# Local-attention layers: the feed-forward one pair of blocks later, its input matmuls behind the value matmuls, gelu behind the copies of the output

## The reference, cut to what matters

```
for i in range(DEPTH):                                     # DEPTH = 6
    x = attn_layer(shift_tokens(x), Wqkv[i], ...) + x
    x = ffn_layer(shift_tokens(x), ln_g[i], ln_b[i], W1[i], b1[i], W2[i], b2[i]) + x

def ffn_layer(x, g, bln, W1, b1, W2, b2):
    mu = x.mean(-1, keepdims=True)
    var = ((x - mu) ** 2).mean(-1, keepdims=True)
    xn = (x - mu) / jnp.sqrt(var + 1e-05) * g + bln
    a, gate = jnp.split(xn @ W1 + b1, 2, -1)               # 341 columns each
    return a * jax.nn.gelu(gate, approximate=False) @ W2 + b2
```

## Time and profile before

| | |
|---|---|
| median of 3 runs | 7343.36 us (7342.56 to 7348.19) |
| profiled execution, own time | 7338.15 us |
| its span, first to last instruction | 7336.3 us |
| stretch of the six layers | about 2741 to 7222 us |
| busy share of the span | PE 75%, DVE 63%, ACT 45%, POOL 36% |
| mean granted TensorE clock | 0.858 |

### The profile page before, as it was taken

One profiled execution on the slowest core, in us unless ns is written; L12 is line 12 of the kernel. 1 busy time (PEld: TensorE's weight loads), 2 busy tenths in 40 slices (PEclk: granted clock), 3 DMA queues, 4 the chain that ended last, 5 costly groups with the idle time before them and its releaser, 6 DMA issues. The chain is left out here.

```text
span 7336.3 us, 228324 instructions
## 1 busy us (share of the span) xinstructions
PE 5478.9 (75%) x94991; PEld 3176.4 (43%) x95226; DVE 4621.9 (63%) x9757; ACT 3311.9 (45%) x6753; POOL 2637.1 (36%) x2351
## 2 busy tenths in 40 slices
PE   5777877454777746888888888888888888888874
PEld 1222222112232214555555555555555555555552
DVE  5666666345555545676676666666666766666764
ACT  1444444121333313555555555555555555555542
POOL 0000000000000005555555555555555555655550
PEclk9999999576898967888888888888888888888885
DMA  3011010002111101001100110011001100110000
GB/s 95 14 20 20 13 20 14 26 0 84 27 20 26 20 8 52 23 23 29 32 23 23 29 32 23 23 29 32 23 23 31 34 23 23 31 29 23 23 19 18
DMA packets 99949, 197.56 MB, mean 27 GB/s; under 512 B 23616, under 2 KB 50048, under 8 KB 99328
## 3 DMA queue, kind: packets, MB, share of 16 engines
q1 hardware_dynamic: 94944, 195.44, 10.3%
q10 hardware_dynamic: 4896, 0.84, 0.1%
HBM read 67.45 MB, written 27.26 MB: 13 GB/s over the span
## 5 line engine op out<-in xcount | busy, mean ns | idle before, releaser
L340 DVE TENSOR_REDUCE a_mpart<-a_pm 128x1 f32<-128x512 f32 (+2 forms) x1904 | 1087.4, 628 | 511.9 <-PE a_pm L412 316.7
L517 ACT ACTIVATE a_probs<-a_ps 128x1024 f32<-128x1024 f32 (+3 forms) x896 | 796.0, 930 | 1123.5 <-PE a_ps L433 856.2
L1219 ACT ACTIVATE w_probs<-w_pa,w_nm,w_rqs 128x64 f32<-128x64 f32 x3072 | 971.2, 415 | 126.3 <-DVE w_nm L1367 124.4
L412 PE MATMUL a_pm<-a_KZ,a_QS 128*128 128x512 bf16 (+3 forms) x1869 | 665.1, 390 | 301.9 <-DVE a_mpart L340 187.7
L1212 ACT ACTIVATE w_sq<-w_pr 128x512 f32<-128x512 f32 x768 | 466.2, 607 | 898.4 <-DVE w_sinb L1355 898.4
L324 POOL COPY a_V<-a_vals 128x288 f32 x32 | 14.5, 452 | 1913.0 <-PE a_po L449 1911.7
L1141 PE MATMUL w_pr<-w_xc,w_w 128*128 128x256 f32 (+1 forms) x1152 | 455.6, 576 | 293.9 <-issue 293.9
L433 PE MATMUL a_ps<-a_QS,a_KS 128*128 128x512 bf16 (+3 forms) x1688 | 514.9, 379 | 140.9 <-DMA a_KS<-k_parts 118.1
L929 POOL TENSOR_TENSOR w_sinb<-w_sinb,w_tabk 128x512 f32<-128x512 f32 x384 | 488.4, 1272 | 283.8 <-DVE w_sinb L1355 283.8
L955 POOL TENSOR_TENSOR w_probs<-w_probs,w_rden 128x512 f32<-128x512 f32 x384 | 392.9, 1044 | 539.0 <-DVE w_rden L1377 539.0
L1355 DVE STREAM_SHUFFLE w_sinb<-w_pr 128x512 f32<-128x512 f32 x768 | 562.6, 733 | 0.0
(11 more groups left out here) (218 smaller groups left out, 10160.9 us busy)
## 6 DMA issues: line engine op xcount, KB each, us to landing
w_Vp<-w_V SPq DMA_DIRECT2D x192, 384.0 KB, 3.7
w_Vp<-w_V SPq DMA_DIRECT2D x192, 128.0 KB, 3.4
a_QS<-q_parts SPq DMA_DIRECT2D x136, 96.0 KB, 3.4
a_KZ<-k_parts SPq DMA_DIRECT2D x136, 96.0 KB, 3.6
a_KS<-k_parts SPq DMA_DIRECT2D x136, 96.0 KB, 3.7
q_parts<-a1p_part SPq DMA_DIRECT2D x48, 128.0 KB, 1.8
k_parts<-a1p_part SPq DMA_DIRECT2D x48, 128.0 KB, 1.8
q_parts<-a2p_part SPq DMA_DIRECT2D x48, 128.0 KB, 1.8
```

The lines of the kernel that those rows point to most:

```text
L340: nc.vector.reduce_max(mpart[:, h, qt, kc:kc + 1], p_m[:, k % 2, 0:width], AX_X).then_inc(max_read, 1)
L412: mm = nc.tensor.matmul(out, QS[:, par, h, qt * P:(qt + 1) * P], KZ[:, par, h, kc * CH:kc * CH + width], start=True, stop=True)
L517: nc.scalar.activation(probs[:, s % 2, 2 * pair:2 * pair + 2, c0:CH], p_s[:, pair, :, c0:CH], ACT.Exp, scale=SM_SCALE).then_inc(exped, 1)
L1219: op = nc.scalar.activation(probs[:, g, t, c, :], s_of(g)[:, t, c, :], ACT.Exp, bias=nm[:, g, t, c:c + 1], scale=scale_of(g)[:, t, c:c + 1])
```

## The change

The feed-forward (`ffn_in`, `gelu`, `gate`, `ffn_out`, `second_residual`) is done for pair n-3 instead of n-2 in turn n; output projection and layer norm stay at n-2. The flag `finish` is split into `mixing` and `feed`. TensorE does `ffn_in` behind `values`, ScalarE does `gelu` behind `keep_out`, and centre, variance, squares and layer norm stand a little later in their orders. A new tile xo keeps the normalized input between the turns; the first residual is written into XS in place of the tile x1, which drops one small instruction and its wait (L1387). vecn holds the two layer-norm vectors apart, with a load of its own. Turn 2 is now written out ahead of the loop, which repeats turns 3 to 93, and a turn 98 is added at the end.

```diff
 def turn(n, attend, mixing, feed, late, early):      # TensorE
     if mixing:
         mix(n - 2, attend)
     if late:
         unit(7, n)
-    if finish:
-        centre(n - 2)
-    if late:
-        norms(n)
-    if finish:
-        variance(n - 2)
-    if late:
-        turn_norms(n)
-    if finish:
-        ffn_in(n - 2, late, attend)
-    if late:
-        turn_back(n, finish)
+        norms(n)
+    if mixing:
+        centre(n - 2)
+    if late:
+        turn_norms(n)
+    if mixing:
+        variance(n - 2)
+    if late:
+        turn_back(n, mixing)
     if attend:
         values(n - 1)
+    if feed:
+        ffn_in(n - 3, 0, late, attend)
+        ffn_in(n - 3, 1, late, attend)
     if late:
-        spread_norms(n, finish)
+        spread_norms(n, feed)
         project_v(n)
-    if finish:
-        ffn_out(n - 2, late)
+    if feed:
+        ffn_out(n - 3, late, mixing)
...
 def spread_norms(m, after_ffn):
-            pe.wait_ge(S[("gl01", "hid2", "hid")[k]], m - 1 + FIRST)
+            pe.wait_ge(S[("gl01", "hid2", "hid")[k]], m - 2 + FIRST)
...
 def turn(n, attend, mixing, feed, late, early):      # ScalarE
     if attend:
         exps(3, 0, n - 1)
         exps(3, 1, n - 1)
-    if finish:
-        gelu(n - 2)
     if attend:
         keep_out(n - 1)
+    if feed:
+        gelu(n - 3)
     if late:
         keep_v(n)
...
 def residual(m):                                     # VectorE
-    dve.wait_ge(S["x2"], m + PPL + FIRST)
-    nc.vector.tensor_tensor(x1[64:128, 0:1], x1[64:128, PAIR:PAIR + 1],
-                            notfirst[64:128, ds(m % PPB, 1)], ALU.mult).then_inc(S["x1p"], 1)
-    dve.wait_ge(S["x1p"], m + 1 + FIRST)
     dve.wait_ge(S["y"], m + 1 + FIRST)
...
+def scale_norm(m):
     dve.wait_ge(S["xn1"], m + 1 + FIRST)
+    dve.wait_ge(S["f2"], m + FIRST)
+    dve.wait_ge(S["vecn"], m // PPL * 16 + 16)
-    nc.vector.tensor_scalar(xc[:, :], xc[:, :], vecs[:, 0:1], vecs[:, 1:2], ALU.mult,
+    nc.vector.tensor_scalar(xo[:, :], xc[:, :], vecn[:, 0:1], vecn[:, 1:2], ALU.mult,
                             ALU.add).then_inc(S["xn"], 1)
...
+    if mixing:
+        var_term(n - 2)
+        layer_norm(n - 2)
     if attend:
         denominator(1, n - 1)
...
-    if finish:
-        gate(n - 2)
+    if feed:
+        gate(n - 3)
+    if mixing:
+        scale_norm(n - 2)
     if late:
         scale_k(n)
```

More of the change, by code:

```diff
@@ L883, in _ @@
                     if l:
+                        sp.wait_ge(S["xn"], m0 + FIRST)
+                        load_n(l)
+                        sp.wait_ge(S["f2"], m0 + FIRST)
+                        load_1(l)
+                    carry_v(m0 + 2)
+                    shift_v(m0 + 2)
+                    if l:
                         sp.wait_ge(S["x2"], m0 + PPL + FIRST)
                         load_2(l)
-                    with sp.Fori(0, PPL - 3) as i:
-                        carry_v(i + (m0 + 2))
-                        shift_v(i + (m0 + 2))
+                    with sp.Fori(0, PPL - 4) as i:
+                        carry_v(i + (m0 + 3))
+                        shift_v(i + (m0 + 3))
                     if l + 1 < DEPTH:
@@ L956, in scale_probs, with turn @@
                                             ALU.mult).then_inc(S[f"pn{g}"], 1)
-                def turn(n, attend, finish, late, early, more=True):
+                def turn(n, attend, late, early, more=True):
                     if late:
@@ L980, in _ @@
                 table_k(1)
[L981 to L987, removed]
+                turn(0, False, True, True)
+                turn(1, True, True, True)
+                turn(2, True, True, True)
+                with nc.Fori(0, PAIRS - 5, engines=bass.OrderedEngineSet([pool.engine]), hint_back_edge=True) as i:
+                    turn(i + 3, True, True, True)
+                turn(PAIRS - 2, True, True, True, more=False)
+                turn(PAIRS - 1, True, True, False)
+                turn(PAIRS, True, False, False)
             @block.tensor
@@ L1125, in variance, with ffn_in @@
                     pe.wait_ge(S["xsq"], m + 1 + FIRST)
-                    nc.tensor.matmul(p_c[:, 0, :], ones[:, :], xsq[:, :], start=True, stop=True).then_inc(S["var"], 1)
-                def ffn_in(m, late, attend):
-                    pe.wait_ge(S["w1"], m // PPL * 16 + 16)
-                    pe.wait_ge(S["xn"], m + 1 + FIRST)
-                    for what, k, bank, at in FFN:
+                    nc.tensor.matmul(p_c[:, 1, :], ones[:, :], xsq[:, :], start=True, stop=True).then_inc(S["var"], 1)
+                def ffn_in(m, part, late, attend):
+                    if part == 0:
+                        pe.wait_ge(S["w1"], m // PPL * 16 + 16)
+                        pe.wait_ge(S["xn"], m + 1 + FIRST)
+                    for what, k, bank, at in FFN[3 * part:3 * part + 3]:
                         if at == 0:
                             if late:
-                                pe.wait_ge(S[("sq7", "n2c", "nrm")[bank]], m + 3 + FIRST)
+                                pe.wait_ge(S[("sq7", "n2c", "nrm")[bank]], m + 4 + FIRST)
                             elif attend:
@@ L1154, in ffn_out, with turn @@
                     mm.then_inc(S["out"], 1)
-                def turn(n, attend, finish, late, early):
+                def turn(n, attend, mixing, feed, late, early):
                     if attend:
```

139 lines of the change are left out of this document (74 added, 65 removed).

## The result

The changed kernel takes 7883.78 us (median of 4 runs, 7879.63 to 7887.56) against 7344.3 for the kernel before beside it: a ratio of 1.0734, 95% interval 1.0718 to 1.075. Slower by 540 us. The forecast was +616 for the profiled execution, which took 549 more: 7887.35, with a span of 7885.5, and the mean granted clock fell from 0.858 to 0.823.

The account below looks back on a forecast made before the run. No engine is full; engines wait for each other in a turn. 44.96 + 5.17 + 1.5 + 0.3 = 51.93, 596 us over 93 turns plus 20: +616, 7960 us; range 7780 to 8110, likeliest case 7870 to 8030.

Parts of the forecast that it names:

- The likeliest case: Whole loop: a turn between 51 and 53 us, forecast total 7960 us; chance 0.55.
- Front half: Ahead of the values: last transposition over at T+27.0, 3.5 of ffn_in's 4.22 us becoming a wait, values ending 0.7 earlier.
- The chain: Behind the values: copies 2.05, table load 1.28, gelu 1.20, gate 1.25, hand-overs 0.2; scale_k 5.17 us later, at T+35.9.
- rival (d): Table load right behind the copies: holds ScalarE longer, at most 1.28 us a turn, 119 more, 8079 us; chance 0.06.
- Ffn_in, 2.85 expected: TensorE behind the values: ffn_in takes 2.85 us, over at T+32.5, hidden behind the table load.
- The clock: TensorE's clock falling behind idle stretches: 1.5 us a turn on project_v, 0.3 on the values.
- what would show it: Signs in the new profile, among them keep_out about 0.7 us earlier, scale_k at T+35.9, a turn of 52 us.
- Rival (b): Between ffn_in and project_v: the clock holds through the thin stretch, turn 50.13 us, total 7792 us; chance 0.2.
- (c): Clock falls both ahead of the values' second half and of project_v: turn 54.03 us, total 8154 us; chance 0.14.
- Behind scale_k: From scale_k to the next turn: 14.23 us, taken as unchanged.
- the forecast's 6.41: Whole loop: new turn 51.93 against the mean 45.52, 6.41 us more a turn, 596 over 93 turns.
- The ends: First turns and last turns outside the steady loop: together 20 us more.

Follow-up runs that it names:

- e7: e5 with GpSimd scaling the first two groups of probabilities ahead of its last rotate: 7228.74 us, ratio 0.9856.
- e10: The changed kernel with only GpSimd's scaling of the first two groups of probabilities moved ahead of its last rotate: 7790.45 us, ratio 1.0617.
- e1: The kernel before with only gelu moved behind keep_out, ffn_in still ahead of the values: 8046.43 us, ratio 1.0958.
- e5: The changed kernel with ffn_in ahead of turn_back and gelu ahead of keep_out, delay by one pair kept: 7453.97 us, ratio 1.0159.
- e2: The changed kernel with the gelu table load ahead of keep_out, gelu itself still behind: 7861.6 us, ratio 1.0708.
- e3: The changed kernel with table load and gelu both ahead of keep_out, ffn_in still behind the values: 7862.9 us, ratio 1.0712.
- e4: The changed kernel with ffn_in back ahead of turn_back and the values, gelu still behind keep_out: 8077.61 us, ratio 1.1003.
- e12: e4 plus six extra matmuls a turn right behind the values, results never read: 7868.72 us, ratio 1.0718.
- e6: The changed kernel with three layer-norm operations moved behind keep_parts: 7854.82 us, ratio 1.0713.
- e11: e7 with e6's move of three layer-norm operations behind keep_parts: 7123.18 us, ratio 0.9712.
- e9: The changed kernel plus eight unread matmuls a turn, five ahead of turn_back, three between the halves of the values: 8171.89 us, ratio 1.1137.

## Why the prediction was right, and which step was off

The likeliest case came, and its main term for its reason: the chain copies, load, gelu, gate stands open behind the values. That the total came within 67 us is partly luck: scale_k stands 0.6 later than forecast, clock included, and what follows it is 1.3 shorter, because the price of the clock came in another place. Step by step:

- **Front half.** The floor was to come at T+17.0 and came at T+16.33; GpSimd was to hold the transpositions, and does: second one over at T+19.83 (forecast T+19.8), turn_back at T+21.92 (T+21.8), last one over at T+26.72 (T+27.0). e7 and e10 show that it is GpSimd's order. The forecast called 3.5 a wait in the middle of the values, though its own times give 2.1 there (T+24.9 to T+27.0); 0.59 came, and 4.70 of idle ahead of them.
- **The chain.** From the start of the copies to scale_k 6.17; the terms of the forecast add up to 6.28, which it wrote as 6.2. e1 puts scale_k equally late with nothing but the move of gelu, and e5 takes it back with nothing but ffn_in and gelu in front. Gelu starts 0.01 behind the end of the load (5054.50 + 1.28, then 5055.79), so rival (d) falls: the load takes 1.28 there as before. Of the drain of about 1380 ns that the Trainium skill gives in ScalarE: Activation LUTs, What ACT_TABLE_LOAD costs, no row shows anything, before or after.
- **Ffn_in, 2.85 expected behind copies and load.** It took 4.10, at half clock until about 5054.8, and is still hidden. That it was nearly the bound itself the forecast did not see; e2 and e3 show it.
- **The clock, the step that failed.** The forecast put 1.5 on project_v and 0.3 on the values. In the turn shown project_v paid nothing (3.67), and the second half of the values 1.0 (3.75 instead of 2.73, which it takes in the turns shown below). So the values ended at T+30.66, 1.0 behind the forecast's T+29.7 (1.0 for the clock and 0.2 for the hand-over to the second half and the copies, less 0.3 for the earlier probabilities), and the copies started later than before (T+30.41), not 0.7 earlier as was said under what would show it. I had argued from the idle between ffn_in and project_v alone. But ffn_in right behind the values is what holds the clock through it, when it starts at half clock and so ends late: e4 without it pays, e12 with other matmuls in its place does not, and e6, where it runs at full clock in its place, pays as well. The term was 1.8, and it measured 1.0, in the one place where I had put 0.3. Rival (b), the clock holding at both places, and (c), falling at both, are each wrong for one of the two places.
- **Behind scale_k.** 14.47 to the next turn instead of 14.23, which the forecast had taken over unchanged. Between scale_k and the second residual it is 0.31 more (6.75 against 6.44), behind it 0.07 less.
- **The mean.** 6.10 for scale_k and 0.24 behind it make 6.34 for the short turn of before; the mean of before is 0.56 longer than that turn, that of after 0.12 longer: 5.90 a turn, 532 in 90 turns. Taken over turns 4 to 92, 5.33 of it lie at scale_k and 0.55 between scale_k and the second residual. At the forecast's 6.41 it would have been 577. The ends were put at 39 for the rest (three more turns at 6.41, and 20) and measured 18.

Of turns 4 to 92, 78 are as described. In the other 11 the clock goes as the forecast said: in six of them, which take 53.1, and more mildly in five, which take 51.6. TensorE in one of the six (from 5175.94), and its window over the second half of the values:

```profile
5205.46 2.85 PE L1152 MATMUL w_pr<-w_xo,w_w 128*128 128x256 f32 x12
...
5213.15 6.43 PE L1071 MATMUL w_pr<-w_wv,w_xg 128*128 128x512 f32 x8
```

```profile
5202.79:5205.52 2.73, 2.73 (x257) 1.00 0.00 0
```

```profile
5221.24 0.48 DVE L1505 SCALAR_TENSOR_TENSOR XS<-w_pc,w_vecs,XS 64x256 f32 x1 [7.04 <-PE w_pc L1165]
```

The last row is VectorE's second residual. The second half of the values is at full clock, the copies start 1.04 earlier, ffn_in is at 2.85, and project_v pays 2.76: the same kernel, the price in the other place, and 1.8 worse for it. In the five milder turns project_v takes 5.0. These 11 turns also explain the changed kernel's mean of 639 ns for a record of project_v, against 601 before.

Open: why the clock rises early, for the second half of the values and with it for ffn_in, in just these turns; and the 0.31 ahead of the second residual, for which see the last section.

## What to carry to other kernels

Before work is moved behind an engine's last burst, look at who waits for its buffers there: here PSUM banks and VectorE's own order, gate ahead of scale_k, tied gelu, gate and the next pair's keys into one chain of 6 us that nothing covered. Room made ahead of a burst is only worth something if its other inputs come earlier too; the same delay by a pair lost 7.3% as built, and with it the kernel gained 2.9% when ffn_in and gelu were kept in front and the orders of GpSimd and VectorE were adapted. And a clock price belongs to a place: work that seems idle filler may hold the clock for the next product on the path, so follow the granted clock of each burst through the whole turn, in each variant.

## What the runs showed of the hardware that I had not expected

- Value matmuls with 32 columns feel the clock less than wide ones: the same 257 records take 2.73 at clock 1.00 and 3.75 at 0.50, 1.4 times as long. The matmuls of 512 columns go from 3.67 to 6.50 for the same eight records, 1.8 times, and the six of ffn_in from 2.85 to 5.46.
- A small product on VectorE can be held by GpSimd. In e7, e10 and e11 every operation of the Newton step that took over 0.3 instead of about 0.2 in the loop ended less than 0.1 behind a product of GpSimd that had started before it, 267 in all; in the kernels before and changed none was stretched. No run isolates it.
- In these runs the fall of the clock mostly moved rather than vanished. Mean records of project_v and of the values (reading w_V), in ns: before 601 and 226, changed kernel 639 and 284, e2 602 and 289, e12 602 and 275, e5 801 and 262, e6 798 and 265, e4 900 and 272, e9 908 and 259, e10 601 and 289. Nearest to the kernel before are the two with the shortest mean turns, e7 with 661 and 230 and e11 with 603 and 248.
- VectorE's queue shows 91 operations ahead of the second residual of the changed kernel (min, median and max in ns). The kernel before has such operations ahead of its first residual, but none at this place:

```profile
L1505 DVEq FUSED_REGOPS  x91: 262/265/267, 2958.3 to 7586.4; - x91
```

  XS is now both read and written there at an address held in registers. The 0.31 lies just there: from the end of ffn_out to the second residual it is 0.35 in the changed kernel and 0.04 before, and every kernel built on the changed one in which project_v takes 3.67 shows 6.73 to 6.76 from scale_k to the second residual. That the queue's operation is the cause is argued from its place and size only. The change also adds a wait there, for centre's matmul, which had long been over; no run took either away.
